# Attention of a hybrid block: 64 items in one unbroken run, and a maximum pass of paired 64-row matmuls

## The reference

```python
# 1. recurrent layer (complex scan over time, two small matrices, gelu, norm)
# f. gated bottleneck layer, before and after the attention: top 32 of 256, softmax, gating
# 2. attention, per batch (T = 1024 rows, 8 heads of 64, latent of 64):
lat = z @ Wkv_down.T                      # T x 64
q   = z @ Wq.T                            # per head T x 64
k, v = lat @ Wk_up.T, lat @ Wv_up.T       # per head T x 64
p   = softmax(q @ k.T * 64 ** -0.5)       # T x T, not causal
x   = x + (p @ v) @ Wo.T
```

## Time and profile before

| what | value |
|---|---|
| median of 3 runs | 1613.02 us (1611.66 to 1614.74) |
| the profiled execution | 1612.51 us, span 1610.8 us |
| busy share of the span | PE 82%, DVE 79%, ACT 69%, POOL 65% |
| granted TensorE clock, mean | 0.935 of full speed |
| chain that ended last | issue 29%, PE 25%, DVE 24%, POOL 9%, ACT 7% |
| DMA | 8 GB/s over the span |

### The profile page before, as it was taken

One profiled execution on the slowest core, in us unless ns is written; L12 is line 12 of the kernel. 1 busy time (PEld: TensorE's weight loads), 2 busy tenths in 40 slices (PEclk: granted clock), 3 DMA queues, 4 the chain that ended last, 5 costly groups with the idle time before them and its releaser, 6 DMA issues.

```text
span 1610.8 us, 37935 instructions
## 1 busy us (share of the span) xinstructions
PE 1325.7 (82%) x10588; PEld 789.8 (49%) x10588; DVE 1278.9 (79%) x2953; ACT 1105.1 (69%) x2389; POOL 1044.0 (65%) x1234
## 2 busy tenths in 40 slices
PE   5888988767666679998799987999879998867675
PEld 2444444434344335656356663566635666444343
DVE  7988887379999669983689936899368994499997
ACT  3433431777777649995499954999549995888885
POOL 3456565258888738883388842888428885078887
PEclk9999999878988799999999999999999999989997
DMA  6000000000000000000000000000000000000000
GB/s 185 27 1 1 0 0 1 1 1 0 0 0 0 1 1 1 0 1 2 1 1 0 0 2 1 1 0 0 2 1 1 0 0 1 1 14 26 13 26 26
DMA packets 16972, 13.54 MB, mean 8 GB/s; under 512 B 5190, under 2 KB 16652, under 8 KB 16908
## 3 DMA queue, kind: packets, MB, share of 16 engines
q1 hardware_dynamic: 16908, 12.67, 2.6%
HBM read 8.47 MB, written 4.19 MB: 8 GB/s over the span
## 4 chain that ended last, share of the span: by engine, by line
issue 29%; PE 25%; DVE 24%; POOL 9%; ACT 7%; DVEq 3%; SPq 1%; DMA 1%; ACTq 1%; POOLq 0%
DVE arena L1319 5%; DVE arena L1219 4%; DVE arena L1214 4%; PE banks L1674 3%; DVE arena L1127 3%; PE banks L1595 3%; POOL arena L653 3%; PE banks L1614 2%; ACT arena L976 2%; POOL arena L648 2%; PE banks L1616 2%; PE banks L1527 2%; DVE arena L1339 2%; ACT arena L983 2%; PE banks L1580 2%
## 5 line engine op out<-in xcount | busy, mean ns | idle before, releaser
L653 POOL TENSOR_TENSOR arena<-arena 128x512 f16<-128x512 f32 x320 | 405.3, 1275 | 85.2 <-ACT arena L976 84.8
L983 ACT ACTIVATE arena<-banks 128x512 f32<-128x512 f32 x512 | 297.9, 595 | 65.9 <-PE banks L1616 56.2
L1319 DVE TENSOR_REDUCE arena<-banks 128x1 f32<-128x1024 f32 x256 | 307.1, 1216 | 19.6 <-PE banks L1595 10.3
L1339 DVE TENSOR_TENSOR arena<-arena 128x512 f16<-128x512 f32 x192 | 202.5, 1056 | 68.6 <-POOL arena L648 62.9
L976 ACT ACTIVATE arena<-arena 128x512 f16<-128x512 f32 x384 | 233.1, 624 | 0.0
L1629 PE MATMUL banks<-arena 128*128 128x65 f16 x2048 | 217.8, 197 | 13.8 <-POOL arena L653 13.7
L1630 PE MATMUL banks<-arena 128*128 128x64 f16 x2048 | 217.8, 193 | 0.0
L1629 PEld LDWEIGHTS banks<-arena 128*128 128x128 f16 x2048 | 192.2, 98 | 51.3 <-POOL arena L653 30.0
L1631 PE MATMUL banks<-arena 128*128 128x65 f16 x2048 | 216.8, 194 | 0.0
L1614 PE MATMUL banks<-arena 128*128 (+1 forms) x512 | 198.5, 388 | 10.8 <-ACT arena L983 10.8
L1219 DVE MATCH_REPLACE8 arena<-arena 128x256 f32<-128x256 f32 x512 | 205.3, 408 | 0.2
(11 more groups left out here) (196 smaller groups left out, 2931.4 us busy)
## 6 DMA issues: line engine op xcount, KB each, us to landing
x<-in_L_attn_a_x SPq DMA_DIRECT2D x8, 512.0 KB, 3.6
out<-x SPq DMA_DIRECT2D x8, 512.0 KB, 2.9
arena<-in_L_attn_a_W_in SPq DMA_DIRECT2D x1, 768.0 KB, 6.2
arena<-in_L_attn_a_W_mid SPq DMA_DIRECT2D x1, 512.0 KB, 6.9
arena<-in_L_attn_a_w_w SPq DMA_DIRECT2D x2, 256.0 KB, 7.1
arena<-in_L_attn_b_Wq SPq DMA_DIRECT2D x1, 512.0 KB
arena<-in_L_attn_b_Wo SPq DMA_DIRECT2D x1, 512.0 KB
fW<-in_L_ffn_weight SPq DMA_DIRECT2D x1, 256.0 KB
```

Of the source, the lines that this page charges most:

```text
L653: nc.gpsimd.tensor_tensor(pr_lo[c][:, kt, :], pr[:, kt, :], pr_hi[c][:, kt, :], ALU.subtract).then_inc(a_lP, 1)
L983: nc.scalar.activation(pr[:, kt, :], ps[6 + kt % 2][:, :], ACT.Exp, scale=SM_SCALE).then_inc(a_P, 1)
L1319: nc.vector.tensor_reduce(mx[c][:, j:j + 1], psum[:, 2 * pair:2 * pair + 2, :].rearrange("p a b -> p (a b)"), X, ALU.max).then_inc(a_mx, 1)
L1339: nc.vector.tensor_tensor(pr_lo[c][:, kt, :], pr[:, kt, :], pr_hi[c][:, kt, :], ALU.subtract).then_inc(a_lD, 1)
```

## The change

Four things are done together.

1. **One run of 64 items.** The loop over batches and the loop over heads are written out. What `project` and the finals did is cut into pieces that stand between the key tiles of the items: item w of a batch (0 to 15) carries, by the tables `FINAL_AT`, `QUERY_AT`, `TURN_AT`, `KEYS_AT` and `LATENT_AT`, one final of the batch before (w = 1, 2, 3, 5, 6, 7, 14, 15), two query products of heads that come 4 items later (w = 0, 4, 8, 12), a piece of the turning (9, 10), the keys (11) or the latents (13) of the next batch. ACT writes the normalised rows of the next batch in w = 7 and 8. PE's pieces stand after S of kt 1 and kt 4, ACT's after kt 3 and kt 6, DVE's after kt 3 and kt 7.
2. **PSUM.** The pieces take banks 2 and 3. The maxima keep banks 0 and 1 alone, so M number j waits for R number j - 1.
3. **The maximum pass.** M is now two matmuls of 64 rows: the first on partitions 0 to 63 for keys 0 to 511, the second on partitions 64 to 127 (a float16 copy of the keys, `kM`) for keys 512 to 1023. The keys' rest is left out of the maximum; the maximum only shifts the exponent, and cancels in the quotient.
4. Keys, latents and outputs have two buffers, queries a ring of 4 heads; statistics of written-out calls go straight to their place, without the copy.

```diff
+        FINAL_AT = {1: 0, 2: 1, 3: 2, 5: 3, 6: 4, 7: 5, 14: 6, 15: 7}
+        QUERY_AT = {0: 1, 4: 2, 8: 3, 12: 4}
+        TURN_AT = {9: 0, 10: 1}
+        KEYS_AT, LATENT_AT = 11, 13
...
-            def max_scores(W, hh, c, j, pair=0, read=None):
-                pe.wait_ge(a_mx, W * MX + (j if read is None else read) + CREDIT["a_mx"])
-                for half in range(2):
-                    last = mm(ps[2 * pair + half][:, :], qA[:, bass.ds(hh, 1), c * CH + j * P:c * CH + j * P + P],
-                              kA[:, half * CH:half * CH + CH], start=True, stop=True)
+            def max_scores(W, j):
+                wait_from(pe, a_mx, W * MX + j)
+                for half, k_half in enumerate((kA[B % 2][0:HD, 0:CH], kM[B % 2][HD:P, :])):
+                    last = mm(ps[half][:, :],
+                              qA[HD * half:HD * half + HD, slot, c * CH + j * P:c * CH + j * P + P],
+                              k_half, start=True, stop=True)
                 last.then_inc(a_mps, 1)
...
+            for W in range(ALL):
                 for kt in range(KT):
+                    if kt % 2 == 0 and W + 2 < ALL:
+                        max_scores(W + 2, kt // 2)
+                    scores(W, kt)
+                    if kt in (1, 4):
+                        c = kt // 4
+                        if w in FINAL_AT and B:
+                            J = (B - 1) * FINALS + FINAL_AT[w]
+                            if c:
+                                out_final(J, 3)
+                            else:
+                                out_turn(J, 2)
+                        if w in QUERY_AT and W + GROUP < ALL:
+                            query(B * GROUPS + QUERY_AT[w], c)
...
+                    if kt in WEIGHTED_AT and W:
+                        weighted(W - 1, WEIGHTED_AT[kt])
+                    if kt == 5 and W + 1 < ALL:
+                        max_row(W + 1)
...
(ACT)
+                for kt in range(KT):
+                    exps(W, kt)
                     if kt - 1 in HIGH_ACT:
+                        high(W, kt - 1)
+                    if kt == 3 and W + 1 < ALL:
+                        max_scaled(W + 1)
+                    if kt in (3, 6):
+                        c = kt // 6
+                        if w in FINAL_AT and B and c == 0:
+                            out_turned((B - 1) * FINALS + FINAL_AT[w], 2)
+                        if w in QUERY_AT and W + GROUP < ALL:
+                            query(B * GROUPS + QUERY_AT[w], c)
...
+                        if w in (7, 8) and onward and c:
+                            attn_rows(B + 1, w - 7)
+                    if kt == 5 and W + 1 < ALL:
+                        max_row(W + 1)
...
(DVE)
+                for kt in range(KT):
+                    if kt % 2 == 0 and W + 2 < ALL:
+                        largest_of(W + 2, kt // 2)
                     if kt in LOW_DVE:
+                        low(W, kt)
+                    if kt in (3, 7):
+                        c = kt // 7
+                        if w in FINAL_AT and B and c:
+                            final((B - 1) * FINALS + FINAL_AT[w], 3)
+                        if w in QUERY_AT and W + GROUP < ALL:
+                            query_low(B * GROUPS + QUERY_AT[w], c)
...
+                if W:
+                    normalise(W - 1)
```

More of the change, by code:

```diff
@@ L683, in _ @@
+            final_rstd(BATCH - 2, 1)
+            for half in range(2):
+                final_rstd(BATCH - 1, half)
             ffn(1)
@@ new lines, in query, with out_turned @@
+            def query(G, c):
+                act.wait_ge(a_qps, G * 2 + c + 1)
+                for odd in range(2):
+                    half = slice(HD * odd, HD * odd + HD)
+                    nc.scalar.activation(qA[half, (2 * G + odd) % Q_RING, c * CH:c * CH + CH], ps[2 + c][half, :],
+                                         ACT.Copy).then_inc(a_q, 1)
+            def out_turned(J, bank):
+                act.wait_ge(a_ft, J + 1)
+                nc.scalar.activation(oT[J % 2], ps[bank][:, :].rearrange("p (a b) -> p a b", a=NH // 2),
+                                     ACT.Copy).then_inc(a_fe, 1)
@@ new lines, in _ @@
+            for k in range(KB2):
+                turned(0, 0, k, k)
+            for k in range(KB2):
+                turned(0, 1, k, 2 + k)
+            for c in range(2):
+                keys(0, c, 4 + c)
+            for c in range(2):
+                query(0, c)
+            for c in range(2):
+                latent(0, c, 6 + c)
+            max_scaled(0)
+            max_row(0)
+            act.wait_ge(f_x, NT + CREDIT["f_x"])
+            for W in range(ALL):
+                B, w = W // ITEMS, W % ITEMS
+                onward = B + 1 < BATCH
@@ L1002, in _ @@
+                    if kt == 5 and W + 1 < ALL:
+                        max_row(W + 1)
+                high(W, KT - 1)
+            for j in range(FINALS):
+                out_turned((BATCH - 1) * FINALS + j, j % 2)
             ffn(1)
@@ L1359, in _ @@
+                if W:
+                    normalise(W - 1)
+            normalise(ALL - 1)
+            for j in range(FINALS):
+                final((BATCH - 1) * FINALS + j, 6 + j % 2)
+            dve.wait_ge(a_fx, NT)
             ffn(1)
@@ new lines, in _ @@
+            pe.wait_ge(s_prep, 4 + CLEARED)
+            for k in range(KB2):
+                turn(0, 0, k, k)
+            for k in range(KB2):
+                turn(0, 1, k, 2 + k)
+            for c in range(2):
+                keys(0, c, 4 + c)
+            for c in range(2):
+                query(0, c)
+            max_scores(0, 0)
+            latent(0, 0, 6)
+            max_scores(0, 1)
+            latent(0, 1, 7)
+            for j in range(2, TPC):
+                max_scores(0, j)
```

581 lines of the change are left out of this document (319 added, 262 removed).

## The result

| what | before | changed |
|---|---|---|
| median | 1612.34 us (1610.45 to 1614.74, 4 runs) | 1711.99 us (1711.36 to 1718.89, 4 runs) |
| the profiled execution | 1612.51 us | 1718.9 us, span 1717.2 us |
| busy share: PE, DVE, ACT, POOL | 82, 79, 69, 65% | 78, 74, 64, 59% |
| granted TensorE clock, mean | 0.935 | 0.917 |

The ratio is 1.0627 [1.0596, 1.0658]: the change costs 6.3%. The forecast was 1686 us with a range of 1560 to 1745 and 0.76 for slower.

What follows compares the result with a forecast made beforehand. PE was taken as the tightest queue within stages, with 186 us lying between them; the change was to add a longer wait loop. 1612.5 - 10 (start) + 78 (items) + 5 (matmul mode changes) = 1686 us, range 1560 to 1745.

Steps and rivals of the forecast that it cites:

- The loop: M1, ahead of kt 2, waits for R0 of its item, closing a loop through PE, ACT, DVE: 10.1 us against 8.9; chance 0.70.
- Pieces inside it: Finals, queries, keys, latents, turned pieces and rows put between key tiles lengthen the loop, to 11.1 to 14.8 us an item.
- P: An item without pieces; 10.1 us forecast.
- F: An item with a final of the batch before; 13.1 us forecast.
- Q: An item with two query products; 14.8 us forecast.
- T: An item with turned pieces; 11.1 us forecast.
- The product's share of F: PE's product waits for ACT's copy ahead of S of kt 5; 2.1 us of an item with a final.
- The pair: Two 64-row maximum matmuls side by side on PE: 0.22 in place of 0.43 us, 0.86 us less PE work an item.
- The gate held: Rival denied: DVE reaches R0 early enough that PE never waits at M1; 1492 us, chance 0.10.
- The pieces did not fill it: Rival denied: most pieces fall into PE's 2.5 us of idling at M1; 1566 us, chance 0.12.
- The sum: The 64 items from first to last score: 827 us against 749, +78, plus 5 for changes between whole-array and 64-row matmuls.
- The start: The first project stage, ahead of the items, keeps 2 of 8 query products: 29 us in place of 39, -10 us.

Runs made afterwards that it cites:

- e1: The kernel before with only the banks of M changed, all maximum matmuls in PSUM banks 0 and 1; 1713.79 us, ratio 1.0641.
- e5: The changed kernel with PE's M moved to ahead of kt 1, 4, 6, 7, DVE's order left; 1597.52 us, ratio 0.9891.
- e11: e1 with its maximum matmuls moved from ahead of kt 0, 2, 4, 6 to ahead of kt 1, 4, 6, 7; 1649.49 us, ratio 1.0226.
- e12: The changed kernel with PE's product with voB moved from behind S of kt 4 to behind S of kt 7; 1669.86 us, ratio 1.0354.
- e9: e5 with ACT's normalised rows of items 7 and 8 put behind the item's last rounding; 1596.03 us, ratio 0.989.
- e10: e5 with the second copies and rests of pieces put at the item's end or the next one's start; 1599.72 us, ratio 0.9913.
- e4: The changed kernel with M moved to ahead of kt 1, 4, 6, 7 and DVE's reductions R moved too; 1636.0 us, ratio 1.0148.

## Why the prediction was right, and where 26 us are missing

- *The loop.* Right in its mechanism, and shown by e1 and e5: the single pair with the gate ahead of kt 2 costs 104 us alone, and moving M away takes 114 us back. e11 shows that the place makes 64 of the 104 us; the other 40 stay at the new place. That the sum of 10.1 us came within 0.13 is in part luck, as said above.
- *Pieces inside it.* Measured, in items with the clock at its upper level, against the forecast: P 10.23 (10.1), F 13.19 (13.1), Q 14.73 (14.8), T 10.92 (11.1), keys 14.49 (14.1), latents 12.23 (12.1), item 8 with queries and rows 16.83 (16.85). The product's share of F is shown by e12.
- *The pair.* The PE work that it saves was mis-sized: 0.22 us in place of 0.43 was taken, 0.32 to the next S and 0.1 ahead of it are right. Two sizes were off against each other: the two changes of 0.1 us take back the 0.21 us that the pair saves. Since the loop and not PE's work set the item, neither showed much in the sum.
- *The rivals.* The gate held. The pieces did not fill it: the mean item is 858.5 / 64 = 13.4 us, above the 11.8 where that rival decides. Moving PE's product (e12) brings the mean item to 12.7 us, which is part of the way.
- *The sum.* From first to last score 1446.2 - 587.7 = 858.5 us; the sum had 827 + 5. The items are thus 31.5 us over their 827, 5 of which the sum had set aside for the changes between whole array and halves. The start gave 8.2 us, not 10. Behind the last score the changed kernel takes 271.0 us where the kernel before took 265.9; that was priced at 0. Some 4 of these 5 us lie in the second bottleneck layer (218.7 us from its first matmul on, 214.6 before, with as many instructions on each engine). In e5 it takes 218.4, and why stays open. The profiled execution lies at the upper end of its four runs, 7 us over the median.

The term that was missing is the clock inside the items. Counted from the reciprocals, the 60 items from w = 2 of the first batch on lie 26.0 us over the forecast. In 17 of them the granted clock is at its lower level, 1.2 GHz, for 3.4 us or more, and these carry 22.5 us; the other 43 carry 3.4 us in sum. The first two items add 4.9, the last two 0.6. Thirteen of the 17 follow a Q item. The first one behind the Q of w = 0 of the second batch, on PE:

```profile
808.22 1.12 PE L1710 MATMUL banks<-ident,xcT 128*128 128x128 f32 x4 [2.63 <-DVE xcT L1403]
809.36 0.61 PE L1740 MATMUL banks<-arena 64*128 64x512 f16 x2
809.89 0.61 PE L1763 MATMUL banks<-arena 128*128 128x512 f16 x1
```

The first final of a batch turns rows that the batch's last `normalise` (L1403) writes, and that one stands on DVE behind the query rest. PE idles for 2.6 us, and then its matmuls take 0.61 us each, the second matmul of S starting 0.41 us behind the first where 0.22 us is usual.

Is it the late start behind a Q item that costs the time, or the clock? The same item settles it, because it occurs three times with different clocks. The latents' item (w = 13) follows a Q item in each of the first three batches; its stretches in batch 0, 1 and 2 (the columns are those of the earlier trace rows; the clock is the third number from the end):

```profile
758.00:771.50 13.50, 11.46 (x140) 7.46 (x140) 8.93 (x11) 8.12 (x18) 7.07 (x9) 0.87 0.01 1
977.40:989.60 12.20, 10.37 (x144) 7.46 (x144) 8.80 (x11) 8.01 (x18) 7.11 (x9) 1.00 0.01 2
1202.00:1217.00 15.00, 13.13 (x144) 8.87 (x144) 9.01 (x13) 8.18 (x18) 7.24 (x9) 0.77 0.01 2
```

It takes 13.56, 12.23 and 14.93 us, and the forecast was 12.1. At full clock, behind a Q item like the others, it is 0.13 us over. The item w = 6 tells the same: 13.25 us at full clock in the third batch, 14.5 in the second and the fourth, at 0.76 and 0.77. The Q items matter in another way: PE idles longest in and behind them, and that is where the clock fell. Of its 18 falls between the first and the last score, 17 lie beside an idle time of PE of 2.0 to 3.8 us. Not every such idle time brought one: four others, of 2.03, 2.09, 2.38 and 3.65 us, did not. Over all items the granted clock is 0.94, where it was 0.99 inside the old stages. Waiting as such does not cost the clock: e1 waits 140 us at M, all but 8 of its 143 waits under 1.42 us, and keeps a mean of 0.934. So the step of the forecast that fell short is a term it left at nothing, the clock in items where PE idles for 2 us and more; by the split above it is worth some 20 of the 31.5 us. No run holds the clock alone; that it carries the excess of the other items too is read from the same split.

## What to carry to other kernels

- When buffers are taken away to make room, find the instruction in each in-order queue that now waits one step less far back, and add up the loop from it through the engines back to itself, once a turn. Here a wait for a reduction one step nearer turned 186 us of gaps saved into 100 us lost, and the busy share fell on every engine.
- The remedy was not the buffer but the place: the same instruction one or two key tiles later in PE's queue, and a product moved to where PE waits anyway, gave 138 us. Move one queue at a time: the version that moved two made a gate of its own.
- A piece moved out of one item's loop is a gain only if it does not stand in the next item's loop; idle time of the engine elsewhere in that item does not help. e9 and e10 gained in the item that was watched, and lost it in the one behind.

## What the hardware showed that was not expected

- Going between whole-array and 64-row matmuls costs 0.1 us each way on top of the matmuls (nothing on the way in where PE had idled), so a side-by-side pair of 512 columns between whole-array matmuls takes 0.42 us, as much as two serial ones (0.43).
- After an idle time of 2.6 us PE's next matmuls of 512 columns started 0.41 us apart in place of 0.22, and the same item took 12.2, 13.6 and 14.9 us at a granted clock of 1.00, 0.87 and 0.77. 140 us of waiting, nearly all in stretches under 1.42 us (e1), left the mean clock where it was.
- The same subtraction on DVE (L) takes 0.68 us, or 1.63 us where POOL's own began just before it: in all 46 long ones of the changed kernel POOL's had begun 0.06 to 0.08 us earlier. Where POOL's began after DVE's, as in 66 others, DVE's took 0.7 us. In e4 a long one lay on the path: R2 stood behind it.
